# ELU of layer 1 moved into its attention, and the seams between the stages of a four-layer graph network

## The reference, cut to what matters

```python
def layer0(inp):                       # attention, the mask is adj > 0
    h = inp @ W
    e = leaky_relu(h @ a[:F] + (h @ a[F:]).T, 0.2)
    pos = softmax(where(mask, e, NEG_INF), 1) @ inp
    neg = -softmax(where(mask, -e, NEG_INF), 1) @ inp
    return elu(concatenate([pos, neg], 1) @ wtrans)
def layer1(x):                         # 8 heads of 64
    nX = heads(x @ W)
    nX = a_ln * (nX - mean(nX)) / (std(nX) + EPS) + b_ln
    kg = leaky_relu(at1 + at2.T, 0.2) * graph
    y = softmax(where(mask, kg, NEG_FILL)) @ nX + nX
    return elu(y)
def layer2(X):                         # hyperbolic linear map, weighted midpoint over adj
    XW = mobius_matvec(W, X)
    return expmap0(relu(logmap0(weighted_midpoint_lincomb(adj, XW))))
def layer3(x):
    node_att = softmax(x @ node_w, axis=0)
    h = x @ edge_w
    edge_att = softmax(where(adj > 0, h @ h.T, NEG_BIG), 1)
    return adj * (node_att * edge_att) @ (x @ weight) + bias
```

## Time and profile before

| | us |
|---|---|
| runs | 2694.39, 2696.12, 2696.39 |
| median | 2696.12 |
| profiled execution | 2692.73 |
| its span | 2690.9 |
| TensorE busy | 2487.0 (92%) |
| VectorE busy | 1990.8 (74%) |
| ScalarE busy | 1733.9 (64%) |

### The profile page before, as it was taken

One profiled execution on the slowest core, in us unless ns is written; L12 is line 12 of the kernel. 1 busy time (PEld: TensorE's weight loads), 2 busy tenths in 40 slices (PEclk: granted clock), 3 DMA queues, 4 the chain that ended last, 5 costly groups with the idle time before them and its releaser, 6 DMA issues. The chain is left out here.

```text
span 2690.9 us, 54431 instructions
## 1 busy us (share of the span) xinstructions
PE 2487.0 (92%) x20735; PEld 1538.0 (57%) x20735; DVE 1990.8 (74%) x3873; ACT 1733.9 (64%) x3185; POOL 40.5 (2%) x53
## 2 busy tenths in 40 slices
PE   7959999999999769999999995789989979999999
PEld 4524444444444449999999994334436735555554
DVE  5759999999997679999999986582247524455684
ACT  3438888888887568988888985851125543444542
POOL 1200000000000000000000000000000000000000
PEclk9979999999999889999999997999999989999999
DMA  4133344433332652111111115102211143434452
GB/s 180 32 112 126 129 140 135 164 130 129 131 111 107 232 188 73 39 39 41 39 29 39 39 28 194 54 23 75 75 51 40 39 133 96 120 107 130 126 141 52
DMA packets 183666, 260.29 MB, mean 97 GB/s; under 512 B 94361, under 2 KB 124889, under 8 KB 177685
## 3 DMA queue, kind: packets, MB, share of 16 engines
q1 hardware_dynamic: 176709, 222.76, 25.9%
q10 hardware_dynamic: 6736, 34.62, 4.0%
HBM read 197.73 MB, written 59.39 MB: 96 GB/s over the span
## 5 line engine op out<-in xcount | busy, mean ns | idle before, releaser
L1715 PE MATMUL m_acc<-m_y,m_b 128*128 128x260 f16 x3696 | 634.2, 276 | 15.9 <-DVE m_b L1503 14.6
L1466 ACT ACTIVATE m_above<-m_u,m_nvs 128x512 bf16<-128x512 f32 (+1 forms) x864 | 519.7, 682 | 52.7 <-DVE m_b L1503 52.0
L1718 PE MATMUL m_acc<-m_y,m_at_late 128*128 128x130 f16 x2352 | 400.4, 221 | 0.0
L1715 PEld LDWEIGHTS m_acc<-m_y,m_b 128*128 128x128 f16 x3696 | 359.7, 97 | 70.8 <-issue 16.5
L1036 PE MATMUL m_acc<-keep_z_hi,m_p_hi 128*128 128x512 f16 x968 | 362.3, 379 | 20.9 <-DVE m_p_lo L853 17.8
L1039 PE MATMUL m_acc<-keep_z_lo,m_p_hi 128*128 128x512 f16 x924 | 350.1, 379 | 0.0
L1041 PE MATMUL m_acc<-keep_z_hi,m_p_lo 128*128 128x512 f16 x924 | 348.5, 377 | 0.0
L1718 PEld LDWEIGHTS m_acc<-m_y,m_at_late 128*128 128x128 f16 x2352 | 231.2, 98 | 0.0
L1718 PE MATMUL m_acc<-m_y,keep_at_early 128*128 128x130 f16 x1344 | 230.6, 222 | 0.0
L732 ACT ACTIVATE m_p_hi<-m_pm 128x512 f16<-128x512 f32 x242 | 150.8, 623 | 84.1 <-DVE m_pm L845 80.3
L1503 DVE TENSOR_TENSOR m_b<-m_above,m_at_late 128x1024 f16<-128x1024 bf16 (+1 forms) x280 | 176.6, 634 | 16.4 <-PE m_acc L1718 6.1
(11 more groups left out here) (386 smaller groups left out, 5610.3 us busy)
## 6 DMA issues: line engine op xcount, KB each, us to landing
edge_a_rows<-adj ACTq DMA_DIRECT2D x40, 704.0 KB, 4.3
m_at<-adjT SPq DMA_DIRECT2D x11, 1408.0 KB
at<-edge_at SPq DMA_DIRECT2D x22, 704.0 KB, 3.9
keep_at_first<-at SPq DMA_DIRECT2D x22, 704.0 KB, 4.0
m_at<-adjT SPq DMA_DIRECT2D x11, 1280.0 KB
m_u<-rows SPq DMA_DIRECT2D x40, 256.0 KB, 3.7
m_at_late<-at SPq DMA_DIRECT2D x3, 2816.0 KB, 13.7
low<-m_lw SPq DMA_DIRECT2D x32, 256.0 KB, 5.6
```

Source lines behind the costliest of these rows:

```text
L1466: act.activation(pair(above, a % RA, nb)[:, i], u[:, g % RU, 0:nb], ACT.Relu, bias=nvs[:, k, 2 * p + i:2 * p + i + 1], scale=STEEP).then_i ...
L1715: pe.matmul(full.rearrange("p l y e -> p (l y e)"), pair(b01, (m // 2) % RB, nb)[:, m % 2, q // 2, half], y12[:, k % 2, j].rearrange("p l ...
L1718: last = pe.matmul(full[:, :, 1, :], at_of(i0 + q // 2)[:, 0, j, half], y2[:, k % 2, j], start=False, stop=(j == T - 2), skip_group_check= ...
```

## The change

It has five parts.

In attention0's last block, ScalarE converts one tile a step for four steps and then two a step, in tile order. In prep1, VectorE's moments of tile 2 and its wait for x come one step later, behind the first split.

In attention1, ELU is done per unit: ScalarE's `exp(g - 2)` at pair 1, a new `elu(g - 2)` on VectorE at pair 3, and the store of y one unit later. b_ln is made 2b + 1 in place of 2b - 1, so that y + 1 is carried. In midpoint2 `plus` and `exp` are gone, `residual` is (y + 1) - 1 + x, there are five groups for four, and the first three loads of x are issued by ScalarE in place of SP.

The softmax over nodes goes from prep3's end into attention3, split into four pieces. Row block 0's mask is loaded and made in prep3 (am0), so attention3 loads mask 1 first; behind it the bias. The transposes of block 0 come after the chunks 2, 3 and 4 of block 1.

```diff
@@ attention0, ScalarE
                 def convert(m):
-                    if m < UNITS - T:
+                    j = m - (UNITS - T)
+                    if j < 4:
                         convert_tile(m)
-                    elif m < UNITS - HJ:
-                        convert_tile(m)
-                        convert_tile(m + HJ)
+                    elif j < 13:
+                        for i in range(2):
+                            convert_tile(UNITS - T + 2 * j - 4 + i)
@@ prep1, VectorE
                 def moments_of(t, b):
-                    if not (isinstance(t, int) and t < 2):
-                        moments(dve, t, b, x_all, stats, mv, std, s, gate)
+                    if isinstance(t, int) and t <= 2:
+                        return
+                    if isinstance(t, int) and t == 3:
+                        here(0)
+                        moments(dve, 2, 0, x_all, stats, mv, std, s, gate)
+                    moments(dve, t, b, x_all, stats, mv, std, s, gate)
...
-                         before=[(t0 - 6, lambda n_c=n_c: here(n_c)) for n_c, (t0, n) in enumerate(CH)]
+                         before=[(-1 if n_c == 1 else t0 - 6, lambda n_c=n_c: here(n_c)) for n_c, (t0, n) in enumerate(CH) if n_c > 0]
@@ attention1, SP
-                    if g > 0:
-                        store_y(g - 1)
+                    if g > 1:
+                        store_y(g - 2)
@@ attention1, ScalarE
+                def exp(g):
+                    nt, t0 = size(g % NB)
+                    act.wait_ge(y_made, g + 1)
+                    act.wait_ge(minus_made, 1)
+                    act.activation(num[:, 0:nt, 0:DH], yo[:, g % 2, 0:nt], ACT.Exp, bias=minus[:, 0:1]).then_inc(e_made, 1)
...
+                        if p == 1 and g > 1:
+                            exp(g - 2)
                         if p == 4 and g > 0:
                             low(g - 1)
@@ attention1, VectorE
+                def elu(g):
+                    nt, t0 = size(g % NB)
+                    dve.wait_ge(e_made, g + 1)
+                    dve.scalar_tensor_tensor(yo[:, g % 2, 0:nt], num[:, 0:nt, 0:DH], 1.0, yo[:, g % 2, 0:nt], ALU.min, ALU.max).then_inc(eone_made, 1)
...
                         make(g, p)
+                        if g > 1 and p == 3:
+                            elu(g - 2)
                         if g > 0:
                             settle(g - 1, p)
@@ midpoint2
-        GROUPS = [(0, 2), (2, 2), (4, 8), (12, 10)]
+        GROUPS = [(0, 2), (2, 2), (4, 4), (8, 6), (14, 8)]
...
-                    sp.dma_start(x_all[:, both(d), :], x_t[:, both(d), :]).then_inc(x_in[d], 16)
+                    if d >= 3:
+                        sp.dma_start(x_all[:, both(d), :], x_t[:, both(d), :]).then_inc(x_in[d], 16)
...
-                def exp(d):
-                    act.wait_ge(plus_made, d + 1)
-                    act.activation(mx[:, both(d), :], mx[:, both(d), :], ACT.Exp, bias=one[:, 0:1]).then_inc(el_made, 1)
...
                 def first():
-                    act.wait_ge(one_made, 1)
-                    for d in range(2):
-                        exp(d)
+                    for d in range(3):
+                        act.dma_start(x_all[:, both(d), :], x_t[:, both(d), :]).then_inc(x_in[d], 16)
...
-                def plus(d):
+                def residual(d):
                     dve.wait_ge(y_in[d], 16)
                     dve.wait_ge(x_in[d], 16)
                     dve.scalar_tensor_tensor(x_all[:, both(d), :], mx[:, both(d), :], -1.0, x_all[:, both(d), :],
-                                             ALU.max, ALU.add).then_inc(plus_made, 1)
+                                             ALU.add, ALU.add).then_inc(x_made, 1)
@@ prep3
+                    if c == 2:
+                        sp.dma_start(a0, dram["adj"][0:P, 0:N]).then_inc(a0_in, 16)
...
+                def mask_first(n):
+                    act.wait_ge(a0_in, 16)
+                    of = slice(n * HALF, (n + 1) * HALF)
+                    act.activation(am0[:, of], a0[:, of], ACT.Copy, scale=BIG, bias=-BIG).then_inc(a0_made, 1)
@@ attention3
         def after_chunk(t):
             last = max(len(EC[t + 1]) - 1, 0)
+            if t == 0:
+                return [2 + g for g in range(len(GROUPS[t]))]
...
-                load_mask(0)
+                sp.sem_inc(a_in, 16)
+                load_mask(1)
+                sp.dma_start(valid[:], dram["valid"]).then_inc(v_in, 16)
                 sp.dma_start(bias[:], dram["bias3"].broadcast_to([P, D])).then_inc(bias_in, 16)
-                load_mask(1)
...
                 exp_upper(0)
+                act.wait_ge(node_link, 1)
+                act.activation(ne[:], nl[:], ACT.Exp, accum_out=gz).then_inc(z_made, 1)
```

## The result

The changed kernel takes 2668.84 us (median of 4 runs, 2666.83 to 2672.22), the kernel before in the same comparison 2696.26 (2694.39 to 2698.32). The ratio is 0.9899, with a 95% interval of 0.9882 to 0.9917: 27.4 us less. The forecast was 2656, 40 us less, with a range of 2640 to 2674. The sign and the range hold; a third of the gain is missing.

A forecast was written before the change was run, and what follows sets the result against it. TensorE, busy 92% of the span, was taken as the bound; -7.4 - 2.7 + 4.5 + 0.7 - 20.5 - 14.6 = -40.0 from the profiled 2692.73 gave 2652.7, or 2656 as a median. Range: 2640 to 2674.

The forecast's parts named there:

- Layer 0's last block: attention0's last block: new conversion order removes TensorE's 5.45 us gap and 1.9 us of slow steps; -7.4 us (6 to 8).
- prep1's start: prep1: split(0) ahead of tile 2's moments brings TensorE's first product 4 us sooner, 1.3 lost at tile 2's normalise; -2.7 us.
- attention1: ELU inside attention1: 48 added Exps and min/maxes delay TensorE 0.45 to 0.65 us a head; +4.5 us (0 to 17).
- The part for VectorE: attention1's unit changes: two elus, 0.7 us, less 0.2 idle and 0.06 to 0.14 to spare; 0.45 to 0.65 us a head.
- The part for ScalarE: attention1: Exps take 2.4 of ScalarE's 10.5 us idle a head; comparisons queued behind have slack, so 0.
- a head takes over 82 us: attention1: stated sign that the forecast is wrong; the forecast had a head at 80.61 + 0.5 us.
- VectorE becomes the bound, 17: Rival, attention1: every elu lands on the path, 17 us in place of 4.5, kernel at 2669; chance 0.15.
- The rival of a falling clock: Rival, attention1's unit changes: elu waits drop TensorE's clock, 1.9 to 2.0 us a drop, up to +96, 2752; chance 0.03.
- The tail: attention1's end: the last unit's Exp and elu run with nothing beside them; +0.7 us (0.5 to 1).
- midpoint2: midpoint2's start: 11 additions, 11 Exps and four table loads removed, products come earlier; -20.5 us (10 to 24).
- attention3: prep3's end and attention3's start: node softmax moved, masks earlier, first product of the weights sooner; -14.6 us (6 to 18).
- about 10.4: attention3: transposes to first product of the weights take about 10.4 us, not 16.1, as two chunks run before the transposes.

The follow-up runs named there:

- e4_w2_queue: Changed kernel with prep1's 1 MB load of w2 issued on ScalarE's queue at step 2, not SP's behind the x loads; prep1 took 114.12 us.
- e6_pool_table: Changed kernel with attention1's min/max on GpSimd as three instructions and attention3's table loaded early; 2691.13 us, ratio 0.9964 to the kernel before.

## Why the prediction was right or wrong, step by step

*Layer 0's last block*: right, -7.6 and -9.5 in two pairs, -7.3 by undoing it alone.

*prep1's start*: wrong in what is late next. The step "then meets the next late thing: tile 2's normalise" named the wrong one. That bound does exist (2.17 us of TensorE's idle time there), but behind it comes the store of c, at 21.2 us, and copy 12 at 52. A wait of 1.10 us for it was in the trace of before and was not read. The gain is 0.

*attention1*: this is the step that failed most. The part for VectorE was near in size, 0.45 to 0.65 us a head from the margins, 0.43 measured (81.04 - 80.61), but by luck. Its own terms, 0.7 less 0.2 less 0.06 to 0.14, give 0.36 to 0.44. And the place is another: without the Exp TensorE loses at pairs 6 and 7 of the last unit and nothing at the head's start, whose pair was read as tight. The waits forecast at pair 7 and pair 0 do come with both instructions in, and make 0.37 of the 1.5. The part for ScalarE was "those have slack where ScalarE idles, so 0", and it measured 0.73 a head alone and 0.25 more together with VectorE's. ScalarE's 10.5 us of idle time in a head were counted as room for comparisons to be late in. But VectorE waited for them already, 11.1 us over the stage in the trace of before; with the Exp it waits 0.51 us in place of 0.21 in unit 4, and has no idle time behind that until it is in the last unit. The sign "a head takes over 82 us" came true, if barely: 82.02. The rival "VectorE becomes the bound, 17" was nearer in its size, and right for one place: in the last unit VectorE has no idle time and TensorE waits for it. But not every min/max is paid for. The rival of a falling clock did not occur: the granted clock is 1.00 from 989.6 us, in the first head, to the stage's end. Its argument, that 4.6 us or more of waiting stood before the slow stretches, doesn't hold for its own rows: the row at 1692.38 takes 0.61 us behind a wait of 0.85.

*The tail*: +0.7 forecast; VectorE's last instruction ends 3.49 us behind the last matmul in place of 2.73, +0.8.

*midpoint2*: right, 16.2 and 20.3 for 19.8. First product at 22.5 for 22.0 forecast, the fourth at 38.1 for 37.4, the thirteenth at 74.1 for 71.2 in the first profile and 71.5 in the second. The first profile has two stretches at a granted clock of 0.50 among these products, of 3.4 us each, from 1682.6 and 1696.2; the second has one, from 1702.2. That is a part of the difference. The queue move gives nothing, as taken (22.15 us with it undone, 22.04 to 22.66 with it). The Trainium skill's "DMA: Bandwidth & Descriptors" says, on issuing engines not being separate DMA queues, that transfers run on the same 16 DMA engines whoever starts them. This agrees, and so does e4_w2_queue, where later stores waited once a load was moved to the other queue.

*attention3*: the steps up to the row maximum were right within 1.4 us, and the new table load took its 1.28 (0.12 us from row maximum to Exp before, 1.54 now, so 1.42 with the handover). The Trainium skill's figure of 2.66 for a switch ("ScalarE: Activation LUTs", what ACT_TABLE_LOAD costs) is not what this place shows. The step "about 10.4" from the transposes to the first product failed: 14.2. Its 16.1 of before held 1.5 us of slow clock besides. It left out that ScalarE's evacuation of a score tile waits for the store of the one three before, with the transposes' copies behind it. With a ring of four it is 10.2, so the 10.4 was the time without that wait.

## What to carry to other kernels

Idle time of an engine in sum is no room for new work if the engine works in order between two others: 10.5 us idle in a head of 80.6 did not take 2.4 of Exps for nothing. Look for the place where a delay can't be made up. Here the work was added to six units and paid for in one, the short one, in which TensorE has half its matmuls and VectorE no wait. Two edits that take work from around it or move it gave back 8.2 of the 11.2 us. And before a wait is blamed, leave the wait in and take the work out: here the wait of 3.4 us was free.

When work is made earlier ahead of a stage that also moves megabytes, look for the first wait on a transfer behind the place, in the trace of before, however short it is: it may mark a time that doesn't move.

## What the runs showed of the hardware

In e6_pool_table GpSimd's instructions on 128x256 float32 took on average 1.47 us for a min with a constant (0.85 to 2.11), 1.14 for a max and an add in one and 0.89 for a sum of two tiles, where VectorE's whole min/max takes 0.42. The min on half of that, 128x128, took 6.09 us in seven of eight cases and 0.53 in the eighth. In the seven, VectorE ran the same nine TENSOR_TENSOR instructions one behind the other; in the eighth it ran nothing. Some of VectorE's own instructions became longer: those that make m_b from m_u and m_at_late at 128x512 from a mean of 0.75 to 0.81 us, those that read keep_at_early in its place not (0.75 and 0.74). No run separates the reasons.

The same kernel had half-pace stretches of TensorE (granted clock 0.50) of 2.9 or of 5.5 us behind the same gap of 2.8 us, from one execution to another. And attention0, the same instructions, took 676.6 us in the first comparison and 683.3 to 685.0 in the ten profiles of the later ones, on four chips; whether that is the chip is open.
